# First cross-attention of a fused four-layer kernel: softmax denominators by token, output products by head, side work handed out in pairs, and a later place for the second batch's context

## The reference

```python
x = x + L0_xattn(layernorm(x), ctx_1024, ...)      # x: (2, 512, 256), ctx: (2, 1024, 256)
lat = layer_norm(latents, ln_lat_g, ln_lat_b)
ctx = layer_norm(context, ln_ctx_g, ln_ctx_b)
q = (lat @ Wq).reshape(b, n, HEADS, DHEAD)         # 16 heads of 64
k, v = split(ctx @ Wkv)
k = apply_rope(k, cos, sin)
attn = clip(einsum('bhnd,bhsd->bhns', q, k) * scale, -11.0, 11.0)
attn = softmax(attn)
out = einsum('bhns,bhsd->bhnd', attn, v).reshape(b, n, INNER)
return out @ Wo + bo
```

## Time and profile before

| | us |
|---|---|
| three timed runs | 2733.48, 2743.35, 2745.49 |
| median | 2743.35 |
| profiled execution | 2738.05 |
| its span, first to last instruction | 2736.2 |

### The profile page before, as it was taken

The page is one execution under the profiler, slowest core; times in us unless marked ns, Lnnn a source line. Parts: engine busy times, 40 slices in busy tenths (PEclk is TensorE's granted clock), DMA queues, the critical chain, the costliest instruction groups (busy, mean ns, idle before and its releaser), DMA issues.

```text
span 2736.2 us, 34539 instructions
## 1 busy us (share of the span) xinstructions
PE 2156.5 (79%) x13832; PEld 1503.8 (55%) x13832; DVE 1378.3 (50%) x2156; ACT 757.8 (28%) x1164; POOL 701.4 (26%) x757
## 2 busy tenths in 40 slices
PE   4898988669948888985986877499678888469994
PEld 3444544359934444433974444399544544368883
...
GB/s 144 25 30 28 28 18 25 13 222 297 275 58 16 8 10 10 9 8 80 186 238 16 20 8 18 137 326 325 95 12 20 11 8 3 26 272 296 293 300 99
DMA packets 96559, 274.66 MB, mean 100 GB/s; under 512 B 14128, under 2 KB 44592, under 8 KB 96016
## 3 DMA queue, kind: packets, MB, share of 16 engines
...
## 4 chain that ended last, share of the span: by engine, by line
PE 54%; DVE 18%; issue 11%; DMA 5%; ACT 4%; POOL 3%; another core or an unknown queue 0%; SPq 0%; DVEq 0%; POOLq 0%; ACTq 0%
PE psum L2118 12%; PE psum L279 9%; PE psum L2141 8%; PE psum L836 5%; PE psum L816 5%; DVE plain L981 4%; DVE plain L1655 3%; PE psum L1485 3%; PE psum L1458 2%; DMA plain<-in_l_en,plain 2%; PE psum L1502 2%; ACT plain L1143 2%; DMA plain<-sorted_x 2%; DVE plain L954 2%; PE psum L874 1%
## 5 line engine op out<-in xcount | busy, mean ns | idle before, releaser
L2118 PE MATMUL psum<-plain 128*128 128x128 f32 x3904 | 494.1, 279 | 10.1 <-DMA plain<-in_l_shared 8.3
L2118 PEld LDWEIGHTS psum<-plain 128*128 128x128 f32 x3904 | 486.2, 196 | 22.1 <-issue 9.4
L279 PE MATMUL psum<-split 128*128 128x256 f32 (+1 forms) x1728 | 384.4, 376 | 76.7 <-DVE split L352 16.6
L279 PEld LDWEIGHTS psum<-split 128*128 128x128 f32 x1728 | 290.1, 213 | 209.9 <-issue 112.7
L2242 POOL DMA_INDIRECT plain<-in_l_ffn,plain x274 | 260.1, 949 | 395.8 <-PE psum L2141 373.3
L2141 PE MATMUL psum<-plain 128*128 128x256 f32 x1160 | 303.1, 384 | 29.4 <-DVE plain L2207 27.1
L1143 ACT ACTIVATE plain<-psum 128x1024 f32<-128x1024 f32 x224 | 227.4, 1023 | 344.0 <-PE psum L836 233.8
L981 DVE TENSOR_TENSOR plain<-plain 128x1024 f32<-128x1024 f32 x200 | 265.6, 1328 | 12.4 <-ACT plain L1143 9.6
L816 PE MATMUL psum<-plain 128*64 128x512 f32 x896 | 242.8, 643 | 33.8 <-DVE plain L988 29.0
L836 PE MATMUL psum<-split 64*128 64x512 f32 x1536 | 234.6, 429 | 37.9 <-DVE plain L954 30.0
L1190 POOL TENSOR_TENSOR plain<-plain 128x512 f32<-128x512 f32 x48 | 68.9, 1435 | 663.0 <-DMA plain<-plain 657.7
...
## 6 DMA issues: line engine op xcount, KB each, us to landing
...
```

What stands on the lines that cost most here:

```text
L279: m = t.e.matmul(out, lhs[x], rhs[y], start=(first and n == 0), stop=(last and n == 2), skip_group_check=skip)
L2118: m = t.e.matmul(K.bank(b)[:, 256 * z + P * f:256 * z + P * f + P], ws[:, f, c0:c0 + 128], xt[:, k, :], start=(f == 0 and k == 0 and z == ...
```

## The change

1. Denominators by token (L0 only). `divide` now takes each 128-token block of `SA` as the stationary operand and one column of ones as the moving one: 8 matmuls 128 x 1 that give an 128 x 8 tile, tokens on partitions. The reciprocal is of 128 x 8.
2. Outputs by head. ACT copies bank 4 undivided into `OT` (`copied`). `output_heads` multiplies each head's 64 rows of `OT` with its 64 rows of `Wo` into a bank of its own, two token blocks per half, 4 matmuls 64-deep and 256 wide per half; DVE adds to `x` with SCALAR_TENSOR_TENSOR (product times 1/denominator plus `x`), 8 of them per step in place of 4 adds. The residual `x` is read and written twice per block.
3. Order within a step's side work: copy, four pieces of preparation (both key halves, query, first values), divide, first half of the outputs, three pieces, second half of the outputs, the rest. Query before values; weight splits last.
4. Pace: in this attention all engines run the side work after odd tiles, two tiles' worth at once, with weights of its own.
5. The second batch's context comes at the end of step 0's side work. All four value pieces of the second batch are prepared in step 1 as before, now in two groups of two.
6. Prologue: two of the four value pieces come after the query; the DVE scaling of the latents is ahead of the sine table's sign; in `vector_late_turn` both scalings stand ahead of both turns (this function is also used by the second attention).

The diff, cut to its core:

```diff
             vector_scaled(v, K, xn, xn, 4 * h, 4 * h + 4)
+    for h in range(2):
...
             weights = [0.5] * (n > 0) + prep[:2] + [1.8] * (n > 0) + prep[2:]
-            if n == 0 and not own:
-                weights = [0.2, 0.2, 1.0, 1.0] + weights
+            if n and not own:
+                v = 1.5 if n + 1 < self.n and self.values(n + 1)[0] else 0.0
+                p = 1.5 if n + 1 < self.n else 0.0
+                v *= 1 + (n == 1)
+                weights = [p, p, p, v, 2.0, 0.9, 0.2, v, 0.2, 0.9, 0.2]
+            elif not own:
+                weights = [1.5, 1.5, 1.5, 0.0, 0.2, 0.0, 0.2, 0.2, 0.4, 0.4, 1.2, 1.2]
             total = max(sum(weights), 1.0)
-            self.pace.append(paced(weights, total, [(kt + 1) / nk for kt in range(nk)]))
+            if own:
+                self.pace.append(paced(weights, total, [(kt + 1) / nk for kt in range(nk)]))
+            else:
+                two = paced(weights, total, [(kt + 2) / nk for kt in range(0, nk, 2)])
+                self.pace.append([x for n in two for x in (0, n)])
...
-            return ([], []) if n == 1 else ([(1, 0), (1, 1)], [(1, x) for x in range(2, self.units)])
+            return ([], []) if n == 1 else ([(1, x) for x in range(self.units)], [])
...
-def side64(n, A, divide, prepare, output, tail, context):
-    if n:
+def side64(n, A, copied, divide, prepare, output, tail, context):
+    g = prepare(n + 1)
+    if A.own:
+        if n:
+            divide(n - 1)
+            yield
+        for _ in range(2):
+            next(g, None)
+            yield
+        if n:
+            output(n - 1)
+            yield
+    elif n:
+        copied(n - 1)
+        for _ in range(4):
+            next(g, None)
+            yield
         divide(n - 1)
         yield
-    elif not A.own:
+        output(n - 1, 0)
+        yield
+        for _ in range(3):
+            next(g, None)
+            yield
+        output(n - 1, 1)
+        yield
+    yield from g
+    if n == 0 and not A.own:
         yield from context
         yield
-    g = prepare(n + 1)
-    for _ in range(2):
-        next(g, None)
-        yield
-    if n:
-        output(n - 1)
-        yield
-    yield from g
     if n == A.n - 1:
         tail()
-def prepare64(n, A, keys, values, split, late, query, own, rowmax, shift):
+def prepare64(n, A, keys, values, split, late, query, own, rowmax, shift, resplit):
...
     before, last = A.values(n)
+    if n and not A.own:
+        query(n)
+        yield
+        for i in range(2):
+            for x in before[2 * i:2 * i + 2] if len(before) > 2 else before[i:i + 1]:
+                values(*x)
+            yield
+            split(n, i)
+            yield
+        if A.steps[n][1] == 1:
+            resplit(A.steps[n][0])
+        yield
+        return
...
         weigh(n, nk - 1)
-        t.emptied_at(4, "divided", K.count("divided", (L, n)))
+        done = "divided" if own else "av_copied"
+        t.emptied_at(4, done, K.count(done, (L, n)))
     def divide(n):
         b = RB.get()
         t.bank(b)
         t.wait_ge("ones", 1)
         t.wait_ge(*A.adds[n, nk - 1])
+        if not own:
+            for i in range(4):
+                for h in range(2):
+                    m = t.e.matmul(K.bank(b)[:, 2 * i + h:2 * i + h + 1], A.SA[n % 2][:, h, 128 * i:128 * i + 128],
+                                   K.ONES[:, 0:1], start=True, stop=True)
+            m.then_inc(*t.up("sums", L, n))
+            K.at["sums", L, n] = b
+            t.emptied_at(b, "recip", K.count("recip", (L, n)))
+            return
         for h in range(2):
             m = t.e.matmul(K.bank(b)[64 * h:64 * h + 64, :], K.ONES, A.SA[n % 2][:, h, :], start=True, stop=True)
         m.then_inc(*t.up("sums", L, n))
         K.at["sums", L, n] = b
         t.emptied_at(b, "recip", K.count("recip", (L, n)))
+    def output_heads(n, half):
+        p = A.steps[n][0]
+        t.wait_ge("av_copied", (L, n))
+        t.wait_ge(f"wo{p % 2}", (L, p))
+        bs = [RB.get(), RB.get()]
+        t.bank(*bs)
+        for i in range(2):
+            q0 = 128 * (2 * half + i)
+            for h in range(2):
+                r = slice(64 * h, 64 * h + 64)
+                m = t.e.matmul(K.bank(bs[h])[:, 256 * i:256 * i + 256], A.OT[r, q0:q0 + 128], K.WO64[p % 2][r, :],
+                               start=True, stop=True)
+        m.then_inc(*t.up("out", L, n, half))
+        K.at["out64", L, n, half] = tuple(bs)
+        for h in range(2):
+            t.emptied_at(bs[h], "x_added", K.count("x_added", (L, n, half, h)))
...
-    run(prepare(0), 1000)
-    context = iter(()) if own else skip_first(tensor_pair(t, K, 1, RB))
+    context = iter(())
+    if own:
+        run(prepare(0), 1000)
+    else:
+        keys(0, 0)
+        keys(0, 1)
+        values(0, 0)
+        values(0, 1)
+        late()
+        query(0)
+        values(0, 2)
+        values(0, 3)
+        context = skip_first(tensor_pair(t, K, 1, RB))
     for n in range(A.n):
-        side = side64(n, A, divide, prepare, output, tail, context)
+        side = side64(n, A, nothing, divide, prepare, output if own else output_heads, tail, context)
         attend(n, side)
         run(side, 1000)
     divide(n)
-    output(n)
+    if own:
+        output(n)
+    else:
+        output_heads(n, 0)
+        output_heads(n, 1)
...
     def divide(n):
+        if not own:
+            if n:
+                v.wait_ge("x_added", v.made["x_added"])
+            v.wait_ge("sums", (L, n))
+            v.e.reciprocal(K.RCP[:, 0:8], K.bank(K.at.get(("sums", L, n), 0))[:, 0:8]).then_inc(*v.up("recip", L, n))
+            return
...
         v.e.tensor_tensor(A.OT, K.bank(4), A.OT, ALU.mult).then_inc(*v.up("divided", L, n))
+    def output_heads(n, half):
+        b = A.steps[n][1]
+        v.wait_ge("biased", v.seen["biased"])
+        v.wait_ge("recip", (L, n))
+        v.wait_ge("out", (L, n, half))
+        banks = K.at.get(("out64", L, n, half), (0, 0))
+        for h in range(2):
+            if h or half == 0:
+                v.wait_ge("x_added", v.made["x_added"])
+            for i in range(2):
+                q = 2 * half + i
+                x = K.X[:, 4 * b + q, :]
+                m = v.e.scalar_tensor_tensor(out=x, in0=K.bank(banks[h])[:, 256 * i:256 * i + 256],
+                                             scalar=K.RCP[:, 2 * q + h:2 * q + h + 1], in1=x, op0=ALU.mult, op1=ALU.add)
+                m.then_inc(*(v.up("x_added", L, n, half, h) if i else v.up("x_added")))
...
             vector_turn(v, K, K.C64, h, K.gain["ctx"], K.TMP2)
+        vector_late_scaled(v, K, K.XL, True)
         v.wait_ge("tab", 16)
         sin = K.TB[:, 1024:2048]
         v.e.tensor_scalar(sin, sin, K.SGN, None, ALU.mult).then_inc(*v.up("tables"))
-        vector_late_scaled(v, K, K.XL, True)
...
+    def copied(n):
+        if n:
+            s.wait_ge("out", (L, n - 1, 1))
+        s.wait_ge("weighed", (L, n, nk - 1))
+        s.e.activation(A.OT, K.bank(4), ACT.Copy).then_inc(*s.up("av_copied", L, n))
     def prepare(n):
-        return prepare64(n, A, keys, values, split, late, query, own_keys, nothing, shift)
+        return prepare64(n, A, keys, values, split, late, query, own_keys, nothing, shift, resplit)
...
         keys(0, 1)
-        for x in range(A.units):
-            values(0, x)
+        values(0, 0)
+        values(0, 1)
         scalar_late(s, K, K.gain["lat"], K.TMP2)
         split(0, 0)
         split(0, 1)
         query(0)
+        values(0, 2)
+        values(0, 3)
```

32 lines of the change are left out of this document (16 added, 16 removed).

## The result

The change made the kernel 1.1% faster: 2711.5 us (median of 4 runs, 2705.58 to 2713.25) against 2739.72 for the kernel before (4 runs), ratio 0.9892 with a 95% interval of 0.9854 to 0.993. The forecast was a saving of 17 us and a median of 2726 in a range of 2709 to 2743; 28 us were measured, and 2711.5 lies near the range's lower end. The spans of the profiled executions are 2711.1 and 2736.2, 25 us apart.

The account below looks back on a forecast made before the run. No engine was full; nearly 3 us per middle step were waits, on DVE and in an exp-clip-sum loop. Savings 9.1 + 3 + 1.5 + 1.5 + 2 = 17 us took the median from 2743.35 to 2726, range 2709 to 2743.

Parts of the forecast that it names:

- The middle steps: Steps 2 to 14 of the first attention: 27.3 us each in place of 28.0, 9.1 us saved over 13 steps.
- the loop: Second half of a step: exp, clip, sum two tiles back, next exp; 2.97 us a round, filled by no engine alone.
- the layout: One middle step worked out from its first scores at 0: exp 4 at 12.2, next first scores at 26.35.
- Rival A: Middle steps: no sum meets POOL in the second half, steps end at 26.35, whole kernel 2714 us; chance 0.25.
- a collision: In middle steps, DVE's sum of tile 2 meets POOL's last key-rotation instruction: about +0.95 us, bounds 0 and 1.1.
- Rival B: Middle steps: PE or DVE takes the place, steps stay at 28.0, whole kernel 2735 us; chance 0.18.
- Rival C: Middle steps: POOL's four rotation instructions meet the sums three times, steps 29.6, whole kernel 2756 us; chance 0.10.
- Step 0: First step, second batch's context moved behind tile 5: 37.7 us against 39.2, so -1.5, bounds -4 and +4.
- the lump: Second batch's context in the first step: statistics, scaling, two POOL parts and turn, as serial as before when moved.
- Step 1: Second step, with two value pieces more: 31 us against 33.89, so -3.
- Prologue: Before the first scores: both scalings first, two value pieces behind the query; -1.5 us, bounds -4 and +2.
- Step 15 and tail: Last step and after: last reciprocal and product gone, denominators 2 us dearer; -2 us, bounds -5 and +2.

Follow-up runs that it names:

- the two kernels: The kernel after with the latents' first turn back between the scalings, 2715.97 us; the kernel after with all value pieces back ahead of the latents' turn, 2704.51 us.

## Why the prediction was right, and where its sizes were off

*The middle steps.* The mechanism was right point by point: exp 4 at 12.1 (forecast 12.2) behind its scores alone; one sum in the loop at 2.28 (2.2), struck by POOL's last instruction; narrow products 1.95 (2.1) and four output products 1.13 (1.0); exp 7 at 23.5 (23.75); PE's wait before the next first scores ends on the key's low half, 0.66 (1 to 1.5). An ordinary step is 27.0 where I had 27.3. The mis-sized term is what DVE has between the sum of tile 3 and the clip of tile 6: reciprocal, four weighted adds and the low part of a key half take 2.5 us there (295.01 to 297.55), not 2.84. The scores of tiles 6 and 7 came earlier as well, at 17.1 and not 17.85, since denominators and first outputs hold PE 2.65 us and not 3.15, but nothing hangs on it: exp 6 waits for DVE's sum (idle 1.42 behind L1062), and in the layout too the clip of tile 6 stood behind DVE's row and not behind exp 6. Over twelve steps the 0.3 make 3.5 us. The rest is step 14, 25.55 for 27.3, another 1.8: the layout was one for all thirteen, and the step without value pieces, long before and short after, was not laid out. Together these are 5.3 of the 7.1 us that the sum of the stretches lacks.

*Rival A* needed a step without a collision: 25.8 when it is taken away, and 26.35 was forecast for it; 0.35 of the difference lie again between exp 5 and exp 7 (7.25 for 7.6). In the kernel after the collision is there in every one of the 13 steps. That the time A named, 2714, lies nearer to the measured one than the forecast's 2726 is luck. *Rival B*, PE as the bound through 64-deep products that don't overlap, is excluded: 8 records of 256 columns take 1.13. *Rival C*, three collisions in the loop, didn't come; two sums are struck in eight steps (21 long sums in 13), but the first of the two delays nothing.

*What the prediction didn't see* is how far the three parts of the change hang together. I worked out the final layout and it held; had the form or the dealing been judged by its own cost (DVE -1.6 us per step for the form, nothing for the dealing), the form would have had the wrong sign and the dealing would have been missed.

*Step 0* was forecast from a layout whose ends were -4 and +4, and came out at -4.5. The mechanism was right (the lump stays serial, and what is won is that step 1's keys run ahead of it), its size was not: it is worth 5.3 us in step 0 and 1.2 in step 1. The dealing in pairs, to which the forecast gave nothing there, is worth 3.1 in step 0 by the kernel without it, and the clock was left out; the two overlap, for together they are more than the whole. *Step 1*: -3.3 for -3. *Prologue*: -2.2 for -1.5; by the two kernels it is -3.7 for the scalings and +2.5 for the value pieces, and the last 1 us stays open.

*Step 15 and tail*: +0.3 for -2, which with a spread of 1.6 for the same code means no gain. I had subtracted the old reciprocal from the open end and counted DVE alone; the zero weights of the last step put the denominators in front of scores that everything else waits for. With the step paced like the others the two together take 41.8, which is 3.2 less than before.
